# A graph network on one core: the second attention layer takes its last 2048 destinations from the edge matrix

## What is computed

```python
def _gat_layer(x, src, dst, W, a_src, a_dst, b, num_nodes):
    H, C = a_src.shape
    h = (x @ W).reshape(num_nodes, H, C)
    al_s = jnp.einsum('nhc,hc->nh', h, a_src)
    al_d = jnp.einsum('nhc,hc->nh', h, a_dst)
    logits = jax.nn.leaky_relu(al_s[src] + al_d[dst], 0.2)
    alpha = _segment_softmax(logits, dst, num_nodes)
    msg = h[src] * alpha[:, :, None]
    out = jax.ops.segment_sum(msg, dst, num_segments=num_nodes)
    return out.reshape(num_nodes, H * C) + b
```

## Time and profile before

| what | us |
|---|---|
| median of 3 runs (7312.23 to 7317.64) | 7316.36 |
| span of the profiled execution | 7334.6 |
| busy in it: TensorE matmul | 6062.9 |
| busy in it: GpSimd | 5086.1 |
| busy in it: VectorE | 3365.6 |
| busy in it: ScalarE | 1425.8 |

### The profile page before, as it was taken

How to read it: one execution, slowest core, us unless ns; L and a number is a source line. 1 busy time by engine, 2 the same in 40 slices (tenths; PEclk the granted TensorE clock), 3 DMA queues, 4 the chain that set the end, 5 groups by cost and what they waited for, 6 DMA issues and landing times. The chain is left out here.

```text
span 7334.6 us, 120792 instructions
## 1 busy us (share of the span) xinstructions
PE 6062.9 (83%) x30188; PEld 4280.8 (58%) x30188; DVE 3365.6 (46%) x13118; ACT 1425.8 (19%) x5109; POOL 5086.1 (69%) x4839
## 2 busy tenths in 40 slices
PE   3888888886728888867877779998899999988997
PEld 2555555555615555556666656665566656665665
DVE  4444444443436666645555544444233323333444
ACT  2333333332201222212222211111000100010001
POOL 3777777777737777757777757665777677767776
PEclk9887888887869999965555569998999999999998
DMA  8988899884324444433333359885999799979996
GB/s 290 217 186 187 183 191 188 185 184 109 93 83 114 117 116 116 116 77 81 82 81 80 83 159 303 284 282 177 308 311 308 240 316 307 303 240 318 312 318 216
DMA packets 767060, 1440.91 MB, mean 196 GB/s; under 512 B 157272, under 2 KB 484876, under 8 KB 764212
## 3 DMA queue, kind: packets, MB, share of 16 engines
q1 hardware_dynamic: 474532, 886.97, 35.9%
q0 software_dynamic: 289936, 523.75, 32.0%
q10 hardware_dynamic: 2304, 26.74, 0.9%
HBM read 1140.97 MB, written 295.98 MB: 196 GB/s over the span
## 5 line engine op out<-in xcount | busy, mean ns | idle before, releaser
L736 POOL DMA_INDIRECT rows<-gcn_rows,index x1632 | 1550.7, 950 | 664.1 <-issue 457.4
L1277 POOL DMA_INDIRECT rows<-gat_rows,index x1568 | 1500.6, 957 | 646.1 <-issue 459.4
L832 PEld LDWEIGHTS bank<-onehots,rows 128*128 128x128 f32 x8704 | 1146.5, 194 | 598.0 <-issue 539.2
L1608 POOL DMA_INDIRECT support<-rows,index x784 | 1218.7, 1554 | 388.0 <-DMA support<-rows,index 188.2
L832 PE MATMUL bank<-onehots,rows 128*128 128x128 f32 x8704 | 1185.4, 279 | 150.0 <-DVE onehots L881 66.5
L1408 PE MATMUL bank<-onehots,rows 128*128 128x128 f32 (+1 forms) x4704 | 949.6, 339 | 325.3 <-DVE rows L1484 325.1
L1408 PEld LDWEIGHTS bank<-onehots,rows 128*128 128x128 f32 (+1 forms) x4704 | 722.7, 203 | 527.2 <-issue 322.2
L844 PE MATMUL dense_bank<-matrix,edge_space 128*128 128x512 f32 x1792 | 891.2, 619 | 0.0
L1747 PE MATMUL rows_bank<-x_window,cross 128*128 128x256 f32 x1568 | 649.8, 506 | 94.9 <-ACT cross L1725 94.2
L736 POOL DMA_INDIRECT rows<-norm,index x544 | 517.0, 950 | 283.2 <-issue 152.9
L844 PE MATMUL dense_bank<-alpha,edge_space 128*128 128x512 f32 x1344 | 671.4, 621 | 13.5 <-DVE acc L899 13.5
(11 more groups left out here) (306 smaller groups left out, 7408.1 us busy)
## 6 DMA issues: line engine op xcount, KB each, us to landing
matrix<-matrix SPq DMA_DIRECT2D x448, 512.0 KB, 3.9
alpha<-matrix SPq DMA_DIRECT2D x336, 512.0 KB, 4.3
matrix<-zeros SPq DMA_DIRECT2D x196, 512.0 KB
edge_space<-gcn_rows SPq DMA_DIRECT2D x588, 128.0 KB
dst_row<-in_dst_flat SPq DMA_DIRECT2D x100, 512.0 KB
source_row<-in_src_flat SPq DMA_DIRECT2D x198, 256.0 KB, 5.3
support<-zeros ACTq DMA_DIRECT2D x16, 1632.0 KB, 28.0
rows<-gcn_rows,index POOLq DMA_INDIRECT x1632, 5.2
```

The costliest lines, as they stand in the source:

```text
L736: nc.gpsimd.indirect_dma_start(rows[:, k, :], None, table, bass.IndirectOffsetOnAxis(ap=index[:, k:k + 1], axis=0),).then_inc(gathered[k], 16)
L832: done = nc.tensor.matmul(by_chunk(banks[h])[:, c, :], rows[:, k, c * P:(c + 1) * P], onehots[:, k, :], start=first and c == 0, stop=final ...
L1277: nc.gpsimd.indirect_dma_start(rows[:, k, :], None, table, bass.IndirectOffsetOnAxis(ap=index[:, k:k + 1], axis=0),).then_inc(gathered[k], 16)
L1608: nc.gpsimd.indirect_dma_start(support[k % COPIES], bass.IndirectOffsetOnAxis(ap=index[:, k // HALF, k % HALF:k % HALF + 1], axis=0), rows ...
```

## The change

1. The second attention layer gets a pass of its own, `dense_attention_pass`. It gathers 34 turns, and takes the last 2048 destinations from the matrix in 196 steps in the turns 1 to 32. The attention weight of an edge is `exp(leaky_relu(a + d) - leaky_relu(top + d))`; split by sign of `a + d` it is a product of a factor of the source, a factor of the destination and `1 + relu(r_src * r_dst - 1)`. So a step needs, for each pair, only the number of equal edges and that Relu. The table is scaled once by the sources' factor and each group's sum by the destinations' one. Per step: `count` (VectorE), `above_one` (ScalarE), `share` (VectorE), one matmul of 65 × 512.
2. The number of equal edges (up to 3) is put into the two top bits of the gate word. For that the gates are divided by 4 (`SHRINK`) and the number shifted by 30. More than 3 equal edges lead to the passes for uneven graphs (`windows_after`). `matrix_value`, `tail_pair`, `near_values` and `totals` hold three values and not two.
3. The gate passes (`packed`) strip the bits first: VectorE writes each step's gate words without them to one of four buffers, and TensorE reads these. The sum is multiplied by 4 when it is added. `steps_used` takes the place of `group_summed`.
4. The blocks are finished in the order of `ends_by_turn`; the ends take a running number `j` beside the block `b`. Four blocks are left for the tail, and the one before them that is pending.

The core of the diff:

```diff
@@ dense_pass @@
+        packed = value == 1
@@ PE @@
+                    if packed:
+                        pe.wait_ge(s.strip_ready, q + 1)
+                    values = stripped[q % STRIPPED] if packed else values_of(n, value)
@@ DVE @@
                             made.then_inc(s.onehot_ready, 1)
+                            for q in strips_after.get((i * RING + k) // BATCH, []) if packed else []:
+                                strip(q)
+                def strip(q):
+                    dve.wait_ge(step_loaded[q % SLOTS], 32 * (q // SLOTS + 1))
+                    if q >= STRIPPED:
+                        dve.wait_ge(s.steps_used, q - STRIPPED + 1)
+                    nc.vector.tensor_scalar(stripped[q % STRIPPED].bitcast(INT32), values_of(q % SLOTS, 1).bitcast(INT32),
+                                            2 ** COUNT_BIT - 1, None, ALU.bitwise_and).then_inc(s.strip_ready, 1)
...
+def dense_attention_pass(nc, g, table, **fields):
+    loops, batches, per_half = g.turns, RING // BATCH, HALF // BATCH
+    total = GROUPS * g.rows
+    spread_over = GROUPS * GROUP_TURNS * batches
+    steps_of = {}
+    for q in range(total):
+        steps_of.setdefault(batches + q * spread_over // total, []).append(q)
...
+                def load_step(q):
+                    if q >= slots:
+                        sync.wait_ge(s.counted, q - slots + 1)
+                    sync.dma_start(matrix[q % slots], by_step[:, q, :]).then_inc(step_loaded[q % slots], 16)
...
+                def above_one(q):
+                    if q >= 2:
+                        act.wait_ge(s.share_ready, q - 1)
+                    nc.scalar.activation(above[:, q % 2, :], ratio[:, low:low + GROUP], ACT.Relu,
+                                         bias=minus_one[:], scale=source_ratio[:, row:row + 1]
+                                         ).then_inc(s.above_ready, 1)
+                for u in range(loops * batches):
+                    if b is not None and not second:
+                        ends.act_own(act, s, number[b], b)
+                    for q in steps_of.get(u, []):
+                        above_one(q)
+                    exponentials(u)
...
+                def step(q):
+                    pe.wait_ge(s.share_ready, q + 1)
+                    nc.tensor.matmul(dense_bank, scaled_table[:, row, :], shares[:, q % 3, :], start=row == 0,
+                                     stop=row == g.rows - 1).then_inc(s.steps_used, 1)
...
+                        multiply(t, k)
+                        if at == BATCH:
+                            shares_of(half + 1)
+                        if b is not None and at == 3:
+                            ends.pe_first(pe, s, number[b], b, 2 * t + 1 + k // HALF)
+                        if late is not None and at == 5:
+                            ends.pe_third(pe, s, number[late], late)
+                        if b is not None and at == 7:
+                            ends.pe_second(pe, s, number[b], b)
+                        if k % BATCH == BATCH - 1:
+                            for q in steps_of.get(t * batches + k // BATCH, []):
+                                step(q)
...
+                def count(q):
+                    dve.wait_ge(step_loaded[q % slots], 16 * (q // slots + 1))
+                    word = matrix[q % slots].rearrange("p (n v) -> p n v", v=2)[:, :, 1]
+                    nc.vector.tensor_scalar(counts[q % 2], word.bitcast(INT32), COUNT_BIT, None, ALU.logical_shift_right
+                                            ).then_inc(s.counted, 1)
+                def share(q):
+                    dve.wait_ge(s.above_ready, q + 1)
+                    nc.vector.scalar_tensor_tensor(shares[:, q % 3, :], above[:, q % 2, :], 1.0, counts[q % 2],
+                                                   ALU.add, ALU.mult).then_inc(s.share_ready, 1)
...
+                        batch_of(u)
+                        turned_onehots(half + 2)
+                        if half % 2 == 0:
+                            add(1, base[0], t * batches + batches, t * 2 + 1)
+                        if late is not None:
+                            ends.dve_divide(dve, s, number[late], late)
+                        batch_of(u + 1)
+                        if half % 2 == 1:
+                            add(0, base[1], t * batches + (batches + HALF // BATCH), t * 2 + 2)
+                        if late is not None:
+                            ends.dve_late(dve, s, number[late], late)
+                            ends.dve_later(dve, s, number[late], late)
```

More of the change, by code:

```diff
@@ L898, in add_group @@
                         here = g.acc[:, c, low:low + GROUP]
-                        done = nc.vector.tensor_tensor(here, here, dense_banks[c][:, 0:GROUP], ALU.add)
+                        sums = dense_banks[c][:, 0:GROUP]
+                        if packed:
+                            done = nc.vector.scalar_tensor_tensor(here, sums, SHRINK, here, ALU.mult, ALU.add)
+                        else:
+                            done = nc.vector.tensor_tensor(here, here, sums, ALU.add)
                     done.then_inc(s.group_added, 1)
@@ L1376, in _ @@
                 pe.sem_inc(s.summed, batches)
-                def shares(i, n):
-                    if not inside:
-                        return
-                    h = n % 2
-                    pe.wait_ge(s.from_window_ready, i * 2 + (n + 1))
-                    pe.wait_ge(share_loaded[h], i * 16 + 16 * (n // 2 + 1))
-                    if not (isinstance(i, int) and 2 * i + n < 2):
-                        pe.wait_ge(s.exponent_ready, i * batches + (n - 1) * per_half)
-                    for k in range(HALF):
-                        done = nc.tensor.matmul(share_banks[h][:, k, :], from_window[:, h, k, :],
-                                                window_share[:, h, :], start=True, stop=True)
-                    done.then_inc(s.shared, 1)
                 def multiply(i, k):
@@ L1519, in turn @@
                     if late is not None:
-                        ends.dve_later(dve, s, late)
+                        ends.dve_later(dve, s, late, late)
                 nc.vector.memset(zeros[:], 0.0).then_inc(s.cleared, 1)
-                for n in range(2):
-                    turned_onehots(0, n)
-                if not folded and inside:
-                    nc.vector.memset(g.z, 0.0)
                 nc.vector.memset(banks[1][:, 0:(chunks + 1) * P], 0.0).then_inc(s.added, 1)
@@ L2032, in _ @@
                 act.wait_ge(s.weighted, 1)
-                nc.scalar.copy(g.tail_pair[:, 0:g.tiles - g.tail + 1, :], g.edge_values[:, g.tail - 1:, 0:2])
+                nc.scalar.copy(g.tail_pair[:, 0:g.tiles - g.tail + 1, :], g.edge_values[:, g.tail - 1:, :])
             @block.tensor
@@ L2157, in degrees @@
         after, totals = psum("after")[:, 0:g.blocks], psum("totals")[:, 0:g.blocks]
-        with phase(nc, "own", "turned", "numbered", "counted", "rooted", "degree") as (block, s):
+        equal = sbuf("equal", [P, g.tiles - g.tail], INT32)
+        most, most_equal = sbuf("most", [P, 1]), sbuf("most_equal", [1, 1])
+        too_many = sbuf("too_many", [1, 1], INT32)
+        across = psum("across")[0:1, 0:P]
+        with phase(nc, "own", "turned", "numbered", "counted", "rooted", "degree", "packed", "most_ready", "most_turned",
+                   ) as (block, s):
             @block.gpsimd
             def _(pool):
+                pool.wait_ge(s.packed, 1)
                 beside(pool)
@@ L2168, in _ @@
                 last.then_inc(s.turned, 1)
+                pe.wait_ge(s.most_ready, 1)
+                nc.tensor.matmul(across, most[:], g.identity[:], start=True, stop=True).then_inc(s.most_turned, 1)
                 pe.wait_ge(s.numbered, 1)
@@ L3278, in build_program @@
         g.matrix_index = part("matrix_index", [P, tiles - g.tail], INT32)
-        g.matrix_value = part("matrix_value", [P, tiles - g.tail, 2])
+        g.matrix_value = part("matrix_value", [P, tiles - g.tail, 3])
         inner, part = scoped()
```

630 lines of the change are left out of this document (472 added, 158 removed).

## The result

| kernel | median of | us | ratio to the kernel before |
|---|---|---|---|
| before | 4 runs (7312.23 to 7318.13) | 7317.0 | |
| changed | 4 runs (7486.31 to 7513.06) | 7497.9 | 1.0251 [1.0236, 1.0266] |

The change costs 181 us. The forecast was slower, by 99 us (7415), in a range from 7270 to 7520. The direction held, and so did the full range; the forecast's own range, 7350 to 7480, did not. The size came out near the rival "the clock stays low" (7514). The profiled execution has a span of 7501.5 us.

The account below looks back on a forecast made before the run. GpSimd's gathers were taken to pace the second attention stage before, VectorE's chain after. Stage +85, gate-pass strips +12 and packing +2 made +99 us on the median 7316.4: 7415 us, own range 7350 to 7480, full range 7270 to 7520.

Parts of the forecast that it names:

- the clock stays low: Rival: TensorE's clock stays low in the second attention layer, turn 36.1 us, 99 us more, 7514; chance 0.2.
- Direction: Whole kernel: slower, as VectorE's chain sets the second attention layer's turn and GpSimd's 20 us sink below it; slower 0.64.
- the sum without ends: VectorE's turn in the second attention layer before block ends: 18.1 us, plus short waits per half of 1.2 to 2.8.
- The stall for `pe_third`: At block ends in the second attention layer, VectorE waits for two tiles, share products and `pe_third`: 3.2 or 6.4 us a block.
- The turn of 33.0: Second attention layer: turn between 30.8 us at full clock and 36.1 at half, taking somewhat over half the time at full speed.
- The rival on the other side: Rival: VectorE reaches the normalising late enough to cover the `pe_third` wait; turn 24.1 us, kernel 7130; turns 24 to 29.4: 0.27.
- The prices: Second attention layer, per step: share 0.68 us, count 0.5, above 0.7; a tail block 8.9 us, five in series.
- Next in line: Second attention layer, after a block's end: VectorE's share waits for ScalarE's `above`, 0.9 us more a block.
- The clock: TensorE's granted clock in the second attention stage after the change: 0.7 to 0.85, against 0.54 before.
- The turns' spread: Second attention layer after the change: equal VectorE instructions of two turns lie 31 to 36 us apart.
- Elsewhere: Outside the second attention stage: 12 us for strips in the three gate passes, 2 us for packing before first matrix writes.
- forecast +85: Second attention stage's sum: 1177 us against 1092, of which 32 turns of 33.0 us make 1056.

Follow-up runs that it names:

- e1: Changed kernel with `pe_third` issued on TensorE ahead of tile 4 and the share products, not behind tile 5: 7380.5 us, ratio 1.0082 to the kernel before.
- e3: Changed kernel with the next block's own rows issued by SyncE at the start of the half, ahead of step loads and `load_half`: 7407.1 us, ratio 1.0124.
- e7: Changed kernel with the 512-column matmul of each step issued twice: 7514.2 us, ratio 1.0258 to the kernel before.
- e11: The kernel of e5 with the 512-column matmul of each step issued twice: 7239.3 us, ratio 0.9883 to the kernel before.
- e4: Changed kernel with gates left undivided, no edge numbers put into them and no strips in the gate passes: 7481.4 us, ratio 1.0220.
- e5: Changed kernel with both the earlier `pe_third` of e1 and the earlier own rows of e3: 7212.3 us, ratio 0.9860 to the kernel before.
- e9: The kernel of e5 with SyncE issuing a half's destinations and shares ahead of the same batch's step loads: 7412.0 us, ratio 1.0127.

## Why the prediction came out as it did

- **Direction: right, for the reason given.** GpSimd's turn sank below VectorE's chain, and its gathers wait for TensorE's sums (511.5 us in 112 places). The three turns with few ends took 22.8 to 25.3 us, where the sum without ends had 20.5 to 23.7 (18.1, and 1.2 to 2.8 for the short waits of each half).
- **The stall for `pe_third`: right in place and range.** 6.0 us a block, in the range of 3.2 to 6.4, near its end at half clock; 252 us in 42 blocks. The turn of 33.0 had taken about 4.5. e1 shows that it is the order on TensorE. The rival on the other side, that this wait is covered, is refuted.
- **The prices: right.** `count` took 0.43 us (taken: 0.5), `share` 0.69 (0.68), `above` 0.80 (0.7), a block of the tail 8.87 (8.9), five of them in series. The Trainium skill (VectorE: DVE Perf Modes, Mode 2×_2P) lets one-operand FP32 instructions on SBUF run at two elements a cycle; the trace agrees for `count` even though it is a shift of 32-bit integers that reads every second word: 512 elements in 0.43 us, where 1024 took 0.75 and the two-operand `share` 0.69 for 512.
- **The step that failed: "Next in line, share(q) of the following half waits for above(q), which ScalarE runs only after the copy of x, the own rows and that normalising: 0.9 us more".** The place was right, the price was not: 147 us and not 44 × 0.9 = 40. I had priced ScalarE's instructions and taken the own rows as landed. I had charged the destinations for standing behind the step loads on SyncE's queue and not followed the queue one entry further, to the load that stands behind the destinations' own wait. e3 removed 114 us of this wait and left 33 us.
- **The clock: too high.** 0.7 to 0.85 was forecast, 0.66 came. The turn measured 35.6 us against 33.0 and 36.1 at half clock, but not by the rival's road: the clock rose over the stage before (0.66 against 0.54), and the number comes from other terms. How much of the 35.6 is the clock stays open, as e7 and e11 leave it. The Trainium skill (TensorE: Matmul & The Clock Gate, What's actually happening) says that activity releases the throttle; the rows of e7 and e11 agree, and only the time does not follow.
- **The turns' spread: wrong.** Equal instructions of two turns were to lie 31 to 36 us apart. The mean fits; the last 23 turns take 38.3 on average.
- **Elsewhere: right in size.** +14 was forecast. Behind the stage the profiled execution is 16.2 us longer, and e4 without strips still 8 longer than before. That the whole rest of the span agrees within 1 us is chance, since 16.6 us went missing ahead of the stage; single executions of the changed kernel differ by up to 27.

As terms over the stage: forecast +85, measured +167. I estimate the difference of 82 us from the rows above. The second wait is 107 more (147 against 40), the stall some 53 more (252 against 44 × 4.5, about 199), and the waits for share products and destinations some 32 more (70 against about 37). Against them, VectorE's own work with its short waits took 21.0 us a turn (1140 less those four waits, over 32 turns) where the sum had 24.1: some 100 less. Together these are some 90, and the estimate is no finer than that. So it is partly luck that the kernel's time came within the full range: an error of some 100 us in VectorE's own work offsets one of 107 in the second wait.

## What to carry to other kernels

Follow a moved or added load through the issuing engine's order, entry by entry: one small load (32 KB) issued behind a wait and two large ones cost 91 us here. Split the idle time of the engine whose chain makes the turn by what ends it: this names what to try, but not what it gives. The two long waits were 252 and 147 us, and curing one alone gave 117 and 91 us. Cure two waits of one chain together before judging either: together they gave 286 us, and turned a loss of 2.5% into a gain of 1.4%.

## What the runs showed of the hardware

- More TensorE work raised its granted clock and hardly the time: some 290 us of added matmuls, clock 0.66 to 0.79, +16 us (e7); some 280 us, 0.76 to 0.88, +27 us (e11).
- A VectorE shift over every second 32-bit word, 512 elements, took 0.43 us, 0.62 of the two-operand instruction of that length.
- The order of DMA issues of one engine moved the kernel by 200 us (e5 to e9) with the same bytes.
